# Queries placed among keys, value rounding on VectorE alone, head and weight scalings moved into the attention, and a second norm taken straight from the residual

## What is computed

```python
q = _fq_sym((layernorm(x) @ Wq + bq) / sqrt(hd), axis=-1)      # per row and head
k, v = split(cond @ Wkv + bkv); k = _fq_sym(k, axis=-1); v = _fq_sym(v, axis=2)   # v: one scale per column, over all keys
attn = _fq_unsigned(softmax(q @ k.T), axis=-1)
x = x + (attn @ v) @ Wp + bp
r = bf16_round(layernorm(x))
h = bf16_round((r - mean) * rsqrt(var + eps) * ln_w + ln_b)
h = gelu(mx_quant(h) @ mx_quant(W1).T + b1); h = mx_quant(h) @ mx_quant(W2).T + b2
out = x + bf16_round(r + h)
# _fq_sym: s = max|x|/127, round(x/s)*s; mx_quant: blocks of 32 with a shared power of two, 8 bits
```

## Time and profile before

| | |
|---|---|
| time, median of 3 runs (lowest, highest) | 2768.71 us (2766.78, 2770.36) |
| the profiled execution's own time | 2770.67 us |
| its span, first to last instruction | 2768.6 us |
| PE busy | 2245.9 us (81%) |
| DVE busy | 2517.8 us (91%) |
| ACT busy | 2045.8 us (74%) |
| POOL busy | 1318.5 us (48%) |
| mean granted TensorE clock | 0.831 of full speed |

### The profile page before, as it was taken

How to read it: one execution, slowest core, us unless ns; L and a number is a source line. 1 busy time by engine, 2 the same in 40 slices (tenths; PEclk the granted TensorE clock), 3 DMA queues, 4 the chain that set the end, 5 groups by cost and what they waited for, 6 DMA issues and landing times. The chain is left out here.

```text
span 2768.6 us, 53001 instructions
## 1 busy us (share of the span) xinstructions
PE 2245.9 (81%) x20020; PEld 1195.2 (43%) x20020; DVE 2517.8 (91%) x3656; ACT 2045.8 (74%) x1884; POOL 1318.5 (48%) x1719
## 2 busy tenths in 40 slices
PE   7999996548888888888788788788887887867876
PEld 3555553214444444444444444444444444433433
DVE  6888777759999999999999999999999999958987
ACT  3555443338888888888888888888888888856665
POOL 2343325105565655555655565565655655652200
PEclk9999998877777776778887778877788788779999
DMA  6555332159999999999999999999999999980000
GB/s 196 130 130 125 92 72 64 56 147 174 184 195 194 181 204 181 195 199 180 204 182 197 193 180 206 186 193 204 175 205 190 190 201 179 175 221 4 19 16 23
DMA packets 1351448, 432.10 MB, mean 156 GB/s; under 512 B 1284212, under 2 KB 1324660, under 8 KB 1350424
## 3 DMA queue, kind: packets, MB, share of 16 engines
q1 hardware_dynamic: 1336344, 382.50, 72.9%
q10 hardware_dynamic: 14944, 47.67, 6.3%
HBM read 73.98 MB, written 37.34 MB: 40 GB/s over the span
## 5 line engine op out<-in xcount | busy, mean ns | idle before, releaser
L828 DVE TENSOR_SCALAR_CACHE_REDUCE arena<-a_ps_s 128x1281 f32<-128x1281 f32 (+1 forms) x1280 | 1824.1, 1489 | 21.7 <-PE a_ps_s L776 14.1
L871 ACT ACTIVATE arena<-arena,a_bias,a_row_scale 128x3328 uint8<-128x3328 f32 (+1 forms) x512 | 1560.4, 3048 | 230.9 <-POOL a_bias L924 230.5
L776 PE MATMUL a_ps_s<-arena,a_q_rep 96*128 96x512 bf16 (+2 forms) x3840 | 1209.2, 436 | 350.8 <-DVE arena L828 309.7
L776 PEld LDWEIGHTS a_ps_s<-arena,a_q_rep 96*128 (+1 forms) x3840 | 312.3, 109 | 787.4 <-DVE arena L828 436.9
L789 PEld LDWEIGHTS a_ps_o<-a_v_head,a_nT 128*128 128x128 f16 x13056 | 527.1, 102 | 254.5 <-issue 141.3
L931 POOL CAST a_nT<-arena 128x1664 int16<-128x1664 uint8 x256 | 402.2, 1571 | 294.0 <-DMA arena<-arena 291.0
L789 PE MATMUL a_ps_o<-a_v_head,a_nT 128*128 128x32 f16 x13056 | 515.6, 183 | 16.7 <-POOL a_nT L932 15.0
L932 POOL CAST a_nT<-arena 128x1664 int16<-128x1664 uint8 x256 | 403.6, 1577 | 0.0
L920 POOL TENSOR_SCALAR a_row_max<-a_row_max,a_part_max 128x1 f32<-128x1 f32 x256 | 92.7, 362 | 426.2 <-DVE arena L828 419.7
L337 PE MATMUL p_ps_k<-p_wkv,p_ctxT 128*128 128x512 f32 (+1 forms) x408 | 185.7, 598 | 0.0
L337 PE MATMUL p_ps_v<-p_wkv,p_ctxT 128*128 128x512 f32 (+1 forms) x408 | 183.4, 592 | 0.0
(11 more groups left out here) (159 smaller groups left out, 1969.9 us busy)
## 6 DMA issues: line engine op xcount, KB each, us to landing
k_parts_transposed<-p_stage SPq DMA_DIRECT2D x25, 768.0 KB, 6.9
p_ctx<-in_ctx_dram SPq DMA_DIRECT2D x25, 512.0 KB, 6.0
arena<-k_parts_transposed ACTq DMA_DIRECT2D x48, 240.1 KB, 4.3
arena<-in_L_ffn_W_dram SPq DMA_DIRECT2D x8, 1024.0 KB, 10.4
arena<-k_parts_transposed ACTq DMA_DIRECT2D x48, 160.1 KB, 3.8
v_integers<-p_ctx ACTq DMA_DIRECT2D x16, 408.0 KB, 2.5
a_v_head<-v_integers ACTq DMA_DIRECT2D x16, 408.0 KB, 4.5
a_q_rep<-q_transposed ACTq DMA_DIRECT2D x48, 128.0 KB, 5.2
```

The costliest lines, as they stand in the source:

```text
L776: last = nc.tensor.matmul(ps_s[:, b, n0:n0 + w], q, k_parts[0:3 * HD, slot, start[c] + n0:start[c] + n0 + w], start=True, stop=True)
L828: nc.vector.tensor_scalar(s_row[:, u, start[c]:start[c] + size[c]], ps_s[:, (u + c) % 2, 0:size[c]], 1.0, None, ALU.mult, ALU.max, accum_o ...
L871: nc.scalar.activation(out, s_row[:, u, keys_of_half[half]], ACT.Exp, scale=row_scale[:, u, 0:1], bias=bias[:, u:u + 1], accum_out=zsum[:, ...
```

## The change

**In `prepare`.** Items of keys and queries form one list: query tiles 0 to 7 come behind key tiles 22, 24, ..., 36, query tiles 8 to 15 behind the last key. The statistics of x are taken from tile 10 on, its second half is loaded during tile 38 into the same buffer and normalised in tiles 45 to 48. The running value maximum is replaced by 13 reductions over groups of tiles that read `arena` with a stride. The weights for keys and values are loaded apart; other loads wait for the first tiles; the bias is split in four steps at tiles 4, 6, 8 and 10. A query is rounded by one product to int8 on DVE and a copy to bf16 on ACT. Values of all heads are rounded by DVE and widened by ACT beside the last six queries; SP stores them. The value scale is turned into a column here.

```diff
+    GROUPS = {8: [(0, 5)], 9: [(13, 18)], 16: [(5, 9)], 17: [(18, 22)], 24: [(9, 13)], 25: [(22, 26)], 29: [(26, 30)],
+              33: [(30, 34)], 37: [(34, 38)], 41: [(38, 42)], 45: [(42, 46)], 48: [(46, 49)], KT - 1: [(49, KT)]}
+    FIRST_QUERY, SECOND_X = 22, 38
+    STATISTICS, PER_TILE = [10, 40], [1, 2]
+    for tile in range(KT):
+        ITEMS.append(("k", tile))
+        if FIRST_QUERY <= tile < FIRST_QUERY + QT and (tile - FIRST_QUERY) % 2 == 0:
+            ITEMS.append(("q", (tile - FIRST_QUERY) // 2))
+    ITEMS += [("q", t) for t in range(HALF_Q, QT)]
...
+        def heads_beside(t):
+            n = t - HALF_Q - 2
+            return range(n * H // 6, (n + 1) * H // 6) if n >= 0 else range(0)
...
-            for h in range(1, H, 2):
-                for part in range(V_PARTS):
-                    some = of_head(h)[:, part * KT // V_PARTS:(part + 1) * KT // V_PARTS, :]
-                    nc.gpsimd.tensor_tensor(some, some, inverse_of(h, KT // V_PARTS), ALU.mult).then_inc(v_scaled, 1)
...
+            for i in range(N):
+                kind, t = ITEMS[i]
+                if i + 1 < N:
+                    turn_in(i + 1)
+                if (kind, t) == ("q", 0):
+                    pe.wait_ge(wq_loaded, 32)
+                project(i)
+                if i >= 1:
+                    turn_out(i - 1)
...
-            def largest_value(t):
-                r = rows(t)
-                dve.wait_ge(vabs_ready, t + 1)
-                dve.wait_ge(vmax_done, t + 1)
-                nc.vector.tensor_tensor(v_scale[0:r, :], v_scale[0:r, :], vabs[0:r, :], ALU.max).then_inc(vmax_done, 1)
+            def largest_values(t):
+                for first, last in GROUPS.get(t, ()):
+                    some = v32[:, first:last, :].rearrange("p t c -> p c t")
+                    dve.wait_ge(v_taken, t + 1)
+                    steps.then_wait(nc.vector.tensor_reduce(largest[:], some, AX.X, ALU.max, apply_absolute_value=True))
+                    steps.then_wait(nc.vector.tensor_tensor(v_scale[:], v_scale[:], largest[:], ALU.max))
...
+                after_first(dve, qi_ready, t)
+                nc.vector.tensor_tensor(heads(q8[:]), qh, over(inv[:], HD), ALU.mult).then_inc(q8_ready, 1)
...
+            for kind, t in ITEMS:
+                if kind == "q":
+                    query(t)
+                    if t == HALF_Q + 1:
+                        scale_of_values()
+                    for h in heads_beside(t):
+                        value_bytes(h)
+                    continue
```

```diff
+            def invert(h):
+                dve.wait_ge(z_ready, h + 1)
+                after_first(dve, scaled, h - 1)
+                nc.vector.reciprocal(zinv[:, h % 2, :], z[:, h % 2, :]).then_inc(z_inverted, 1)
...
             for row in range(ROWS):
+                if row >= QT and row % QT == INVERT_AT:
+                    invert(row // QT - 1)
                 row_of_scores(row, row % 2)
...
+            def scale_head(h):
+                pool.wait_ge(o_taken, (h + 1) * QT)
+                pool.wait_ge(z_inverted, h + 1)
+                of_head = attn[:, :, h * HD:(h + 1) * HD]
+                nc.gpsimd.tensor_tensor(of_head, of_head, over(zinv[:, h % 2, :], HD), ALU.mult).then_inc(scaled, 1)
```

```diff
-                dve.wait_ge(hf_ready, k + 1)
-                steps.then_wait(nc.vector.tensor_tensor(hf[:, k % 2, :], hf[:, k % 2, :], ln_w, ALU.mult))
-                nc.vector.tensor_tensor(h[:, k % 2, :], hf[:, k % 2, :], ln_b, ALU.add).then_inc(h_ready, 1)
+                i, s = (k // 2 + 1) % 2, 2 + k % 2
+                steps.then_wait(nc.vector.scalar_tensor_tensor(hf[:], resid[:, k, :], mv[:, i, s, 0:1], ln_w,
+                                                               ALU.subtract, ALU.mult))
+                nc.vector.scalar_tensor_tensor(h[:, k % 2, :], hf[:], rstd[:, i, s:s + 1], ln_b,
+                                               ALU.mult, ALU.add).then_inc(h_ready, 1)
```

More of the change, by code:

```diff
@@ L147, in prepare @@
         rest1 = ph.sb("rest1", [P, C])
-        vabs = ph.sb("vabs", [P, C])
+        largest = ph.sb("largest", [P, C])
         parts = ph.sb("parts", [P, 3, C], BF16)
@@ L368, in _ @@
                 for half in range(2):
-                    if piece_at(t, 4 + half) is not None:
+                    if kind == "k" and piece_at(t, 4 + half) is not None:
                         turn_weights(piece_at(t, 4 + half), half)
-            def turn_x(t):
-                pe.wait_ge(xn_ready, t + 1)
-                pe.wait_ge(cT_copied, KT + t)
-                for j in range(CC):
-                    last = nc.tensor.transpose(ps_c[:, j, :], x_tile(t)[:, j * P:(j + 1) * P], identf[:])
-                last.then_inc(cT_ready, 1)
@@ L1235, in _ @@
                 take(g_tiles[1])
-                for s in range(2):
-                    hidden(h_tiles[s])
                 for s in range(2):
```

527 lines of the change are left out of this document (257 added, 270 removed).

## The result

The changed kernel takes **2732.83 us**, median of 4 runs (2731.41 to 2735.98); the kernel before, beside it, 2769.53 us (2766.78 to 2771.33). The ratio is 0.987, 95% interval 0.9853 to 0.9887. It is faster, as forecast, but by 37 us and not by 72, and 2732.8 lies above the range's end of 2728. The profiled execution's span is 2729.6 us, 39.0 less than before.

What follows compares the result with a forecast made beforehand. PE was taken to bound the key part, DVE the attention (transfers close behind), both nearly the last stage. First stage -58, attention +6, last stage -20 sum to -72; 2770.7 - 72 - 2 gives 2696 us, range 2670 to 2728.

Steps and rivals of the forecast that it cites:

- Start: Start of the first stage: first projection near 9.5 us, projection 3 near 36; -13 us.
- Tail: Last key to attention: 73.5 us instead of 164.8, the last six queries on DVE alone; -91.
- Attention: Attention and its tail: longer by 6 us, bounds +1 and +23.
- the reciprocals: Attention: one 128x16 reciprocal per head on DVE, 15 x 0.3 us, +4.5.
- the last product: End of the attention: the last head's product on POOL stands open, +1.4 us.
- Last stage: Last stage: earlier start and shorter pairs of tiles, near 31 us instead of 33.9; -20 us together.
- slowing beside POOL: Last stage, DVE's loop over a pair: operations no longer slowed beside POOL's products, 1.2 us less.
- VectorE beside it: Key part: DVE's new work beside PE, late in tiles 8 to 11, 17, 25 and 29; +8 us, bounds +2 and +20.
- On average it hides: Key part: DVE's sum of 342 us lies under PE's 431 us.
- 38 were given: Key part: eight queries among the keys, 4.8 us each on PE, +38 us, bounds +34 and +70.
- Rival B: Key part: strided reduction costs about twice contiguous, 29 us more on DVE, some 12 passed on; 2708 us, chance 0.23.
- Rival D: Key part: queries do not hide, each leaving PE another handoff behind DVE's 3.95 us chain; +28, 2724 us, chance 0.12.

Runs made afterwards that it cites:

- old_norm: The changed kernel with the second norm put back: ScalarE normalises, VectorE multiplies and adds; 2747.74 us, ratio 0.9921.
- even_order: The changed kernel with ScalarE copying out before waiting for POOL, groups of three moved out of tiles 8 to 14, bias split spread over tiles 4 to 16; 2702.20 us.
- contig: The changed kernel with the 13 value-maximum reductions reading contiguous columns instead of hopping from tile to tile (that part of the result changed); 2721.6 us, ratio 0.9824.
- pieces_one_source: The changed kernel with each 2048-column weight product replaced by a one-source reduction of the same duration and a 32-column product; 2718.6 us, ratio 0.982.
- the depth: Three runs on the changed kernel, turning and copying out the item two back: alone 2732.6 us, with ScalarE's order changed 2712.0, with groups of three 2715.4.
- groups3: The changed kernel with the value maximum reduced in 15 groups of three tiles and 3 of two, none beside a weight piece; 2713.3 us, ratio 0.9792.
- tiny_pieces: The changed kernel with the two 2048-column products of each weight piece cut to 32 columns and nothing in their place; 2718.6 us, ratio 0.9816.

## Why the prediction was wrong in size

**Start: right.** Projection 3 at 36.89 us, forecast 36; the first one came at 11.40 and not near 9.5, but of the two tiles costed at the slow clock only the first eight matmuls ran slow (5.82 us). **Tail: right**, 72.8 against 73.5: the last six queries are VectorE's alone, as costed. **Attention: not resolved.** +2.0 for +6 by the two profiles, but the same code took 1862.0 to 1869.3 us in the thirteen profiles of the kernel after and its variants, with a median of 1865.0, or +3.4. The terms of 4.5 us for the reciprocals and 1.4 for the last product are neither confirmed nor refuted. **Last stage: right**, pair at 30.82 (forecast 31), down projection at 3.4 (forecast 3.6); old_norm shows that the norm's way over ScalarE was 2.8 of a pair's 3.1 us, as the forecast's reason had it, and that the 1.2 us "slowing beside POOL" that I took off VectorE's loop as a part of its own was worth 0.3. That the pair still came out so near is in part luck: the forecast gave POOL's part 1.2 us instead of 0.3, and the norm 1.7 instead of 2.8.

**Key part: the step that failed** is "VectorE beside it": its "On average it hides", and its +8. In place of the 8 us PE idled 34.4, and its work then ran 9.0 us longer at a lower granted clock, for which the forecast had no term. The sums themselves were near: the queries cost PE 38.3 us more (even_order) where 38 were given, and VectorE was busy 360 us where 342 were. It was the overlap that was wrong, in three things, and the clock besides. (Cover is the time that PE works on something else while an item is on its way over the other engines.)

First, a term was mis-sized. The reductions were priced contiguous, and cost 1.83 ns a column, 17 us more in all. The Trainium skill's figure (Vector Engine (DVE) Microarchitecture Reference, section 5.2, Measured stream behaviour on trn2: 1.73 ns a column when one source hops 4 KiB at every element and the other streams are contiguous) was right to within 6% for groups of four and five, with hops of 2 KiB here, and not for two and three. I had quoted it and let the contiguous row decide. Rival B had this mechanism, and its 12 us look like contig's 11.8, but that is luck: it gave them to 29 us more on VectorE, where 17 came, and partly to tiles 25, 29 and 33, where contig gained nothing; and its sign, a four-tile reduction over 4 us, did not show at 3.75.

Second, a duration was taken as fixed that the change itself moves. I had read POOL's first subtraction at its 1.16 us of before. In the kernel before VectorE waited behind `take_values` for the absolute values; with the running maximum gone it goes straight on to the piece's product, which so falls on that subtraction. Before, the second one was the slow one (a mean of 1.77 us, L306), and the sum of the two has hardly changed (2.93 us to 3.00). But ScalarE waits in order for the first, with the copies of the input and of the turned parts queued behind it, and for the second only PE waits. Without the slowing 15.6 us return (pieces_one_source), and no rival had it. The two subtractions of the kernel before:

```profile
L306 POOL TENSOR_TENSOR p_parts<-p_rest,p_parts 128x512 bf16<-128x512 f32 x50 | 88.7, 1773 | 37.0 <-ACT p_parts L426 37.0
L303 POOL TENSOR_TENSOR p_rest<-p_kq,p_parts 128x512 f32<-128x512 f32 x50 | 57.9, 1158 | 249.1 <-ACT p_parts L421 249.1
```

Third, cover was counted as an average: 431 - 342 us over the stage. PE's cover is an item's own 7.2 us of projection, and only 3.6 where a query follows. A query does not just add its price, it halves the cover of the tile ahead of it. In the trace each of the eight waits of PE in the queries' stretch stands right behind a query's projection, ahead of the turning of the key before it (L403), three of them over 1 us (2.45, 6.64 and 5.80). That a query's short projection is the reason is read from this place and from the depth's 5 to 8 us; no run varies the projection alone. Rival D was near it, but its sign, a wait ahead of the query's own transposes, did not show, and its "4 us for each query" holds only with a piece at hand: in the kernel after it is 20.9 us from query to query in the two steps without a piece (behind tiles 32 to 36), which is the forecast's price although a group of four is reduced in tile 33, and 23.0 to 27.3 us in the five before.

And the clock: the four waits over 4 us were each followed by work at a lower granted clock (0.81 from 119 to 126 us, 0.74 from 195 to 205, 0.50 from 278 to 282 and 0.76 from 327 to 340; above, 4.55 us for 3.60), so that they cost more than their length. Before, PE never waited in this stretch and its clock stayed at 1.00. No single edit returns the 35 us of the miss (11.8, 12.8 and 15.6 us, 21.1 for groups3). Smaller, better placed groups and the copies' place in the queue together bring back 28.5 us; with the bias split spread and the groups moved once more it is 32.8, but these 4.3 us are little more than two profiles of one code differ by. POOL's subtraction is as slow in even_order as before (a mean of 1795 ns), with PE busy 418 of 429 us: once the copies don't stand behind it and VectorE isn't late, most of it is under cover.

```profile
L344 POOL TENSOR_TENSOR p_rest<-p_kq,p_parts 128x512 f32<-128x512 f32 x50 | 89.8, 1795 | 274.9 <-ACT p_parts L454 274.9
```

What of it still shows there was not tried apart. Why the queries' stretch kept its 19 us without the reductions' hops also stays open.

## What to carry to other kernels

Count cover per item, not per stage, and take an inserted item's shorter work as the cover of the one ahead of it. Before you remove a wait, ask what the freed engine will start at that moment and which engine it will slow; a duration read in the old trace holds only while its neighbours stay. In an in-order queue put what needs nothing ahead of what waits.

## Of the hardware

- A VectorE reduction that hops 2 KiB at each element costs 1.21 and 1.25 ns a column with two or three elements to an output, and 1.83 and 1.82 with four or five; contiguous, 1.19, 1.14, 1.12 and 1.10 (L584 and L585 in after, contig and groups3). The jump between three and four I had not expected; its cause is open.
- A VectorE product of two sources, 2048 columns long, stretches a 512-column POOL subtraction from 1.16 to 3.19 us when it starts just ahead of it (after, L603 and L343), while a reduction of one source and 2048 columns leaves it at a mean of 1.18 (pieces_one_source). A conversion of one source and 2560 columns stretches it too, by 0.57 us in an overlap of 0.72 (tiny_pieces, L539). What tells these operations apart was not tried.
- PE waited 6.64 us in the kernel after and then had a granted clock of 0.50 for at least 3.9 us; eight projection matmuls took 4.55 us instead of 3.60, and twelve transposes 1.46 instead of 0.83 (L403 at 278.08 and at 266.73).
